# Moving twelve weight-casting DMAs of the GpSimd queue from the projection stage into the attention stage

## What is computed

```python
h = _layernorm(x)                                   # x: (4, 4096, 1024) f32
q, k, v = h @ Wq + bq, h @ Wk + bk, h @ Wv + bv     # 8 heads of 128 in each
scores = einsum('bngh,bmgh->bnmg', q, k) / 32
probs = softmax(scores, axis=-1)                    # over the last axis: the 8 heads
x = x + einsum('bnmg,bmgh->bngh', probs, v)
h = _layernorm(x)                                   # then xr, xk: mixes with the previous token
r = sigmoid(xr @ W_r); k = square(relu(xk @ W_k))
x = x + r * (k @ W_v)
```

## Time and profile before

| | us |
|---|---|
| median of 3 runs | 1815.36 (1815.22 to 1855.34) |
| the profiled execution's own time | 1816.18 |
| its span, slowest core (7) | 1814.6 |
| spans of the 8 cores | 1779.6 to 1814.6 |
| stage 1 of core 7 ends, attention starts | about 560 |
| attention of core 7 ends | about 1545 |

### The profile page before, as it was taken

One profiled execution on the slowest core, in us unless ns is written; L12 is line 12 of the kernel. 1 busy time (PEld: TensorE's weight loads), 2 busy tenths in 40 slices (PEclk: granted clock), 3 DMA queues, 4 the chain that ended last, 5 costly groups with the idle time before them and its releaser, 6 DMA issues.

```text
span 1814.6 us, 33694 instructions; the slowest of 8 cores (1779.6 to 1814.6 us)
## 1 busy us (share of the span) xinstructions
PE 1216.2 (67%) x9912; PEld 792.7 (44%) x9912; DVE 1160.9 (64%) x1864; ACT 963.0 (53%) x1504; POOL 107.2 (6%) x136
## 2 busy tenths in 40 slices
PE   3767088888884666666666666666666564478898
PEld 2434044444443444444444444444444453345554
DVE  3564022222223888888888888888888874557875
ACT  1333022222224887888878788787887864112121
POOL 1002000000000000000000000000000000000000
PEclk6777599999996999999989999999999977689999
DMA  9029923333316554554645455464564569421011
GB/s 240 1 41 109 143 62 64 57 56 73 77 60 186 164 175 140 167 171 140 191 143 157 141 182 156 144 191 139 158 182 140 172 206 118 65 53 47 27 45 59
DMA packets 157149, 219.61 MB, mean 121 GB/s; under 512 B 54064, under 2 KB 127920, under 8 KB 154736
## 3 DMA queue, kind: packets, MB, share of 16 engines
q0 software_dynamic: 48320, 96.48, 23.7%
q1 hardware_dynamic: 108656, 120.98, 23.3%
HBM read 197.51 MB, written 36.44 MB: 129 GB/s over the span
## 4 chain that ended last, share of the span: by engine, by line
DVE 53%; PE 21%; DMA 12%; issue 9%; ACT 2%; DVEq 2%; SPq 1%; ACTq 0%; POOL 0%; POOLq 0%
DVE arena L576 18%; PE stAB L230 14%; DVE scratch L536 10%; DVE scratch L541 6%; DVE scratch_f L544 6%; DMA vtspill<-scratch 6%; DMA arena<-vtspill 2%; PE ctxP L268 2%; DVEq L91 2%; DMA wa<-wv 1%; DMA arena<-kspill 1%; DVE x_res L634 1%; PE stAB L877 1%; PE stAB L898 1%; PE stAB L839 1%
## 5 line engine op out<-in xcount | busy, mean ns | idle before, releaser
L604 PE MATMUL ctxP<-arena 128*128 128x128 bf16 x4352 | 305.0, 225 | 292.5 <-DVE arena L576 260.8
L604 PEld LDWEIGHTS ctxP<-arena 128*128 128x128 bf16 x4352 | 261.9, 101 | 361.5 <-issue 360.9
L484 PE MATMUL stAB<-arena 128*128 128x256 bf16 (+1 forms) x2304 | 347.1, 280 | 84.0 <-ACT arena L523 36.7
L230 PE MATMUL stAB<-arena,wa 128*128 128x512 bf16 (+1 forms) x1344 | 319.5, 396 | 21.7 <-DMA wa<-wv 11.1
L484 PEld LDWEIGHTS stAB<-arena 128*128 128x128 bf16 x2304 | 199.5, 102 | 170.5 <-issue 150.7
L576 DVE TENSOR_TENSOR arena<-arena,scratch 128x2048 bf16<-128x2048 bf16 (+1 forms) x192 | 224.5, 1169 | 31.3 <-PE ctxP L604 9.7
L230 PEld LDWEIGHTS stAB<-arena,wa 128*128 128x128 bf16 x1344 | 135.7, 103 | 181.5 <-issue 58.6
L257 DVE TENSOR_SCALAR scratch<-scratch,cvecsb 128x512 bf16<-128x512 bf16 (+1 forms) x104 | 36.5, 351 | 260.0 <-ACT scratch L253 260.0
L523 ACT ACTIVATE arena<-stAB 128x1024 bf16<-128x1024 f32 (+1 forms) x192 | 188.1, 980 | 17.6
L253 ACT ACTIVATE scratch<-stAB 128x512 bf16<-128x512 f32 (+1 forms) x104 | 59.4, 573 | 259.2 <-PE stAB L230 191.8
L512 ACT ACTIVATE arena<-stAB 128x1024 bf16<-128x1024 f32 (+1 forms) x192 | 184.7, 962 | 13.6 <-PE stAB L484 13.5
(11 more groups left out here) (67 smaller groups left out, 1116.5 us busy)
## 6 DMA issues: line engine op xcount, KB each, us to landing
arena<-kspill SPq DMA_DIRECT2D x72, 1024.0 KB, 6.3
arena<-vtspill POOLq DMA_DIRECT2D x72, 1024.0 KB, 7.7
kspill<-scratch SPq DMA_DIRECT2D x8, 1024.0 KB, 5.6
vtspill<-scratch SPq DMA_DIRECT2D x8, 1024.0 KB, 9.5
out<-x_res SPq DMA_DIRECT2D x8, 1024.0 KB, 4.0
qspill<-scratch SPq DMA_DIRECT2D x8, 544.0 KB, 2.9
arena<-qspill POOLq DMA_DIRECT2D x8, 512.0 KB, 11.0
xtmp<-x POOLq DMA_DIRECT2D x15, 256.0 KB, 4.1
```

Source lines behind the costliest of these rows:

```text
L230: r = e.matmul(ps[:, 0:w], wa[:, (g % 2) * 3072 + wi * 1024 + cj * 128: (g % 2) * 3072 + wi * 1024 + (cj + 1) * 128], arena_ap(cj * 4096 + ...
L484: r = e.matmul(stAB[:, g * w:(g + 1) * w], arena_ap(KQ0 + par_k * 4096 + g * 512 + mcq * 128, [[1, 128]]), arena_ap(qbase2 + g * w, [[1, w]]),
L604: r = e.matmul(ctxP[:, reg * 128:(reg + 1) * 128], arena_ap(UB0 + par_u * 2048 + g * w + nt * 128, [[1, 128]]), arena_ap(VQ0 + par_k * 409 ...
```

## The change

The twelve calls of `emit_wcast` leave the loop over `t` and go to the loop over `slot`: one at the head of every eighth slot from 120 to 208, ahead of `stage_loads` of that slot. The DMAs themselves, their semaphore and the waits on it are the same.

```diff
@@ -372,8 +372,6 @@
         emit_tr_evac(t - 1)
         if t + 1 < NT:
             emit_ln_tile(t + 1)
-        if t >= 8 and t % 2 == 0 and (t - 8) // 2 < 12:
-            emit_wcast((t - 8) // 2)
         done = 0
@@ -667,6 +665,8 @@
             vec_op(wts, "v_self", op)
 
     for slot in range(NIT + 4):
+        if 120 <= slot < 216 and slot % 8 == 0:
+            emit_wcast((slot - 120) // 8)
         if slot < NIT:
             stage_loads(slot)
             stage_st(slot)
```

## The result

The changed kernel takes 1788.24 us in the median of its ten runs (1778.77 to 1830.46) against 1815.29 us before. The ratio is **0.9835, 95% interval 0.981 to 0.986**. In some runs of either kernel one half of the chip has a lower TensorE clock and is a few per cent longer; the ratios here, and the ranges in the experiments, leave those executions out. 0.9835 of 1815.29 us is 1785.3 us, 1.8 us above the forecast. The gain of 1.4 to 1.9% is clear of the noise, and under 2%.

The account below looks back on a forecast made before the run. A cast burst flooding the DMA engines was taken to delay the first group's V write; VectorE paces attention. 1816.18 - 40.1 + 8.0 = 1784.1 us profiled, less 0.8 for the median: 1783.5 us, range 1773 to 1797.

Parts of the forecast that it names:

- The burst: End of the first head group in projections: 12 casts leaving together delay the V write; moving them removes 40.1 us.
- Nine casts cost nothing: Attention quads without a Q load: DMA engines busy 11.3 of 12.7 us with a cast, so these nine cost 0.
- the rival of disturbed quads: Attention: casts also make V or K of the nine other quads 2 us late, 18 us on top, 1801 us; chance 0.15.
- Three casts make Q late: Slots 128, 160, 192: a cast ahead of Q makes it 3.9, 4.5 and 4.1 us late; 8.0 us lost in all.
- my signs of being wrong: First boundary stays long, `ctx` waits for V in the nine other quads, or Q lands within 12 us behind a cast.
- What of it is hidden: Late Q in attention: the pipeline hides 1.46 us of a wait, from core 2 at slice 3 (1.0 of 2.46 lost).
- The price of a cast: Time one cast adds on the DMA engines: 4.4 us, from landings in the burst; bounds 3.4 and 6.4 us.
- my upper bound: Price of one cast in attention: at most 6.4 us, its tail sharing engines with the next quad's K load.
- The skill's rule on descriptors: GpSimd DMA issue beside VectorE's fast mode: each Q another 2.5 us late, 7.5 in all, sum 1791; trace doesn't show it.

## Why the prediction was right, and where it was off

- *The burst.* Right. I gave 40.1 us; the first V load of attention comes 38.7 us earlier. The missing 1.4 us are in the boundary: without casts the first group is followed by 48.9 us and not by the 47.6 of the next one. It was right for core 7, the core it was read from; core 4 had lost only about half as much to the burst (19.2 us earlier now).
- *Nine casts cost nothing.* Right. The casts four slots later show it directly (slices of 109.3 to 109.6 us with and without them), and the rival of disturbed quads falls. The DMA share of a quad with a cast and no Q load is 0.93 (core 4, 921.5 to 934.2 us), a little over the 0.85 to 0.9 I gave.
- *Three casts make Q late.* Right in mechanism, place and count: TensorE waits for Q at slots 128, 160 and 192, and moving either the casts or the Q loads away is worth 0.005 of the time, some 10 us. One of my signs of being wrong did appear: 3 of the 24 Q loads behind a cast landed within 12 us of issue (10.8, 11.7 and 11.8). Two of them are on cores where Q needed 9.0 and 8.3 us before; the third, on core 7, was delayed by 0.4 us only.
- *What of it is hidden.* Right: 1.46 us were forecast from a single wait of core 2; measured are 1.5, 1.7 and 1.1, and 1.5 per wait with two casts (core 6: 36.5 us waited, 32.0 lost). That one wait gave so good a value is luck in part.
- *The price of a cast.* Right in the mean: I took 4.4 us from the burst, and over the eight cores Q comes 3.8 us later behind one cast and 8.5 behind two. For the core that counts it was too small: on core 4 Q lands after 18.6, 17.3 and 14.0 us, and before the change after 11.9, 11.4 and 11.0, so 6.7, 5.9 and 3.0 us later, 5.2 in the mean. The waits I gave as 3.5 to 5 us are 8.0, 6.7 and 3.5 there. The worst price lies just above my upper bound of 6.4.
- *Whose price counts.* This is the step that was missing. I worked out the lateness for core 7 with its usual Q loads and got 8.0 us. The mean over the eight cores agrees: 7.9 us more for the three slices. Core 7 itself loses only 3.4, because its Q loads come 3.0, 0.4 and 2.6 us later, and core 4 loses 14.1. The metric takes the slowest core. Why the same cast delays Q by 0.4 us at slice 5 of core 7 and by 6.7 at slice 4 of core 4, no run here shows. That the sum came out within 2 us is in part luck: the profiled execution itself was forecast at 1784.1 and took 1778.8 us, because the slowest core of before had 13.4 us more of V waits at the end than the new slowest core has.
- *The skill's rule on descriptors.* I read it too widely. The Trainium skill (SBUF — State Buffer, Who interferes with whom) ties it to VectorE operations with a two-port mode, and the same section says that `tensor_tensor` has none; the 3.1 us was measured beside a `tensor_copy`. In attention VectorE runs TENSOR_TENSOR (lines 534, 539, 542 and 574), apart from some statistics at the slices' ends, so the page does not forecast the 7.5 us. The trace agrees: V loads are issued in 0.88 us and the casts in 0.53 us in attention, as in the earlier trace rows, and twelve casts that keep clear of Q cost nothing there.

## What to carry to other kernels

When transfers without waits stand behind something that waits, they all leave at once, whatever spacing the program text gives them; look at when they are issued, and compare a disturbed repetition of a loop with its undisturbed neighbour for the price. Before putting background traffic into a quiet stage, look for the one transfer there whose landing already equals its deadline, and either keep clear of it or issue that transfer earlier. Where the metric is the slowest of several cores, a delay that varies costs nearer its worst case than its mean (14.1 against 7.9 us here).

## What the runs showed of the hardware that I had not expected

A load lands later when another transfer is issued right behind it on the same queue, although it was first. With the casts four slots later, from 900 to 1260 us on all eight cores, the 96 V loads with a cast right behind them land after 9.7 us in the median (8.1 to 13.4), and the 90 with nothing behind after 8.3 (6.4 to 12.9). In the kernel before it is 10.5 us with a Q load behind and 7.9 without. Three V loads of core 1 show it at its clearest, the first with nothing behind it, the others with a cast behind (issue, then landing in us):

```profile
L460 POOL DMA_DIRECT2D arena<-vtspill x1: 882/882/882, 926.1 to 926.1; - x1
...
DMA to landing us min/median/max: 7.9/7.9/7.9
...
DMA to landing us min/median/max: 11.1/11.1/11.1
...
DMA to landing us min/median/max: 13.4/13.4/13.4
```

So the two seem to be served in part together and not strictly in turn. Why, no run here shows, and for a Q load with a cast behind it the effect was too small to see. And the sharing between two queues is far from even. Of the eight Q writes (0.5 MB each, SP queue, core 7 of the kernel before) the first, beside the burst, landed 30.9 us after issue, and the median is 2.9 us:

```profile
DMA to landing us min/median/max: 2.7/2.9/30.9
```

The Trainium skill's page DMA: Bandwidth & Descriptors, section Queues, rings and completion order, has each engine take turns between its queues packet by packet. Equal turns would not by themselves give a factor of ten; the packets of a cast may take much longer to serve, or the bursts of the other cores may hold up all of them, and no run here tells these apart.
